# Packed blocks (100 sorted and 320 gathered steps a pass) and three loads of one-hot rows issued by ACT in the norm

## The chip, the core and the metric

The kernel runs on one core of a Trainium2 chip. The metric is the time of one execution on the device in microseconds. Before the change three runs gave a median of 2686.7 us (2684.65 to 2692.53). The profiled execution is a run of its own; profiles below are of it.

## What is computed

A graph of 3125 nodes with 128 features and 50000 edges, sorted by destination (the low nodes have far more edges than the high ones). First five steps of a gated graph network with residual and layer norm, then three edge layers with a residual and a layer norm:

```python
def _gnn_layer(edge_index, x, edge_attr, norm, We, be, Wn, bn):
    src, dst = (edge_index[0], edge_index[1])
    parts = [x[src], x[dst]]
    if edge_attr is not None:
        parts.append(edge_attr)
    e = jax.nn.relu(jnp.concatenate(parts, axis=-1) @ We + be)
    msg = e * norm[:, None] if norm is not None else e
    agg = jax.ops.segment_sum(msg, dst, num_segments=x.shape[0])
    x_new = jax.nn.relu(jnp.concatenate([x, agg], axis=-1) @ Wn + bn)
    return (x_new, e)
...
x = _layernorm(x + _L0_gnn_ref(x, ...))     # 5 gated steps, messages over the same edges
x = _layernorm(x + _L1_gnn_ref(...))        # three _gnn_layer; the edge rows e feed the next
```

## The kernel before, in words

The nodes lie in 25 windows of 128. The edge list is cut into 416 steps of 128 edges. The first 112 steps (`SORT_STEPS`), which hold edges of the crowded low windows, are sorted on the chip into blocks, one block for each pair of a source window and a destination window; the other 304 steps stay as they are. Every stage is a block of its own, with its work written out per engine; semaphores (`wait_ge`, `then_inc`) order it.

**Tables** (`step_tables`, `sort_on_dve`, `sort_on_pe`, 0 to 70 us). DVE and PE work out, for each edge of the 112 steps, its place among the blocks. A block takes whole tiles of 128 places. PE adds the first place of the block for each edge with 25 products in `row_of` (L543), DVE multiplies by the mask of the edge's block (L336) and sums over the windows (L340). The lists of windows of the 152 tiles (`SORT_TILES`) go to `list_i`.

**Adjacency** (`build_adjacency`, 70 to 375 us). POOL scatters a record of each edge of the sorted steps to its place in DRAM (L625), one scatter a step, in the pace of PE's products of the adjacency. Then five gated steps (`gated_steps`, to 940 us) and the norm (`add_and_norm`, to 965 us).

**First node stage** (`node_stage`, 965 to 998 us). It makes the node products P and Q of the first edge layer, kept in SBUF in three bfloat16 parts, P also in DRAM (`p_dram`). Here SP also loads the tables (L1236), and `hot_all`, the destinations of the gathered steps broadcast to all partitions, in four chunks (`load_hot`, L1225; quads 0, 8, 24, 48 and 76 bound them), the first of them ahead of the node products, the other three behind the stores of P. The rows of the sorted tiles are turned (L1287) and stored in `sorted_rows`.

**Edge pass** (`edge_pass`, three times, 998, 1560 and 2158 us). A slot is a quad of four tiles or steps, in the order sorted, gathered, gathered, and so on: 38 sorted and 76 gathered slots. For a slot

- POOL gathers the rows of P of a gathered quad from DRAM, four indirect DMAs (L1496), into one of seven row buffers (`ROW_SLOTS`); for a buffer that was used it waits for the slot sum that read it (`summed`, of L1607). SP loads `pair_rows` of a sorted quad (L1511), and in passes 1 and 2 the edge rows of the pass before (L1516).
- PE makes the edge rows in PSUM: Q by one-hot products of three parts (L1585), for a sorted slot also P (L1578), in passes 1 and 2 the edge rows by w_c (L1589).
- DVE adds the gathered rows (L1714), ACT takes the relu (L1657).
- PE turns the rows (L1600; ACT takes them at L1663, SP stores them at L1536, passes 0 and 1 only) and sums them into windows with weighted one-hots (L1607); DVE adds these sums to the window's column of `agg_t` (L1721).
- DVE makes the one-hots: `pair_hot` from bytes (L1695), `hot_all` in place (L1688, first pass), `hot_w` (L1705).

PE's order is the products of slot q, then turn and sum of slot q - 1. DVE's order is the add of slot q (or the `pair_hot` of the next sorted slot), then per tile the sum of slot q - 1 (L1721) and the weighted one-hot of slot q + 1 (L1705). PE and DVE load the window numbers of three slots at a time into registers. Behind the slots a loop treats tiles that didn't fit into the 152; its body runs once though there are none (L1503 gathers for it). The node stage of the layer follows.

The pace of a gathered slot is in these lines:

```python
def lists(i, first, engine):
    ...keep["list_i"][0:1, i, first:4 * QUAD]...
for q in range(SLOTS):
    if q % 3 == 0:
        values = lists(q // 3, 0, mybir.EngineType.PE)
    products(q, values)
    if q >= 1:
        turn_and_sum(q - 1)
```

## Time and profile before

| | us |
|---|---|
| median of three runs | 2686.7 |
| the profiled execution's own time | 2711.26 |
| its span in the trace | 2709.1 |
| tables | 0 to 70 |
| adjacency | 70 to 375 |
| gated steps and norm | 375 to 965 |
| first node stage | 965 to 998 |
| edge pass 0, with its loop for the rest | 998 to 1515 |
| edge pass 1 | 1560 to 2110 |
| edge pass 2 | 2158 to 2669 |
| last norm | 2669 to 2709 |

The node stages of 45 us lie between the passes. Over the span PE is busy 78%, DVE 53%, POOL 39%, ACT 25%; the mean over stages with such different work says little of any of them. How to read the rows below: a row of a timeline has its start, its length, engine, line and operation, tiles, a count, and in brackets the idle time of the engine ahead of it with what ended it; a row of groups has the busy time, the mean in ns, the idle time and the releaser. "issue" is time in which the engine waited for nothing that the profile shows.

### The profile page before, as it was taken

To read this page: it belongs to the slowest core of one execution; us is meant where nothing else is said; L and a number is where in the kernel's file an instruction comes from. 1 tells how busy PE (TensorE), PEld (TensorE's weight loads), DVE (VectorE), ACT (ScalarE), POOL (GpSimd) and SP (SyncE) were. 2 spreads that over 40 slices of the span, in tenths; PEclk is the share of its full clock that TensorE was granted. 3 is DMA by queue.
4 is the path that set the end of the run, shared out by engine and by line. 5 is a ranking of instruction groups with operands and counts; after the bars stand their busy time and mean duration, and the time that the engine had idled before them with its cause. 6 is when DMAs were issued, how large, how long until landed. Compare 5 with 4: busy or idle time off the path is not lost. (4 is left out here: it accounts for less than half of the span.)

```text
span 2709.1 us, 50361 instructions
## 1 busy us (share of the span) xinstructions
PE 2123.5 (78%) x14516; PEld 1514.4 (56%) x14516; DVE 1447.8 (53%) x4548; ACT 675.5 (25%) x1344; POOL 1068.0 (39%) x1086
## 2 busy tenths in 40 slices
PE   7777769999999726777777558888889458888885
PEld 5112124444444425666776348877878357777773
DVE  6888751322323255666666425555556336566565
ACT  0245751221212131222222312222222301111111
POOL 0544410000000035666664165555553266666650
PEclk7667779999999867889788769999999679999997
DMA  2023560000000043434443135555554134444431
GB/s 80 21 59 72 88 64 1 0 0 0 0 0 0 24 175 116 119 115 118 116 117 110 46 107 166 167 166 166 170 168 159 53 88 115 117 118 117 120 110 38
DMA packets 188937, 242.82 MB, mean 90 GB/s; under 512 B 53218, under 2 KB 115069, under 8 KB 188077
## 3 DMA queue, kind: packets, MB, share of 16 engines
q1 hardware_dynamic: 155852, 179.60, 22.9%
q0 software_dynamic: 32864, 60.32, 9.3%
q8 instruction: 135, 2.21, 0.3%
q14 instruction: 86, 0.70, 0.1%
HBM read 150.92 MB, written 69.26 MB: 81 GB/s over the span
## 5 line engine op out<-in xcount | busy, mean ns | idle before, releaser
L1496 POOL DMA_INDIRECT rows<-p_dram,src_i x912 | 899.4, 986 | 561.1 <-PE psum L1607 230.5
L1721 DVE TENSOR_TENSOR agg_t<-psum,agg_t 128x128 f32 x1368 | 390.8, 286 | 493.9 <-PE psum L1607 208.2
L1589 PE MATMUL psum<-w_c,before 128*128 128x128 f32 x1824 | 419.3, 310 | 18.9 <-issue 18.6
L882 PE MATMUL psum<-adj,parts 128*128 (+2 forms) x1750 | 340.0, 352 | 5.3 <-ACT agg L961 4.4
L1705 DVE TENSOR_SCALAR hot_w<-col_f,dst_loc,weight 128x128 f32<-128x128 f32 x912 | 323.9, 357 | 0.3
L1657 ACT ACTIVATE rows<-rows 128x512 f32<-128x512 f32 x228 | 143.6, 630 | 720.1 <-DVE rows L1714 459.7
L1585 PE MATMUL psum<-q_parts,hot_all 128*128 x2736 | 283.4, 221 | 29.3 <-issue 28.4
L1589 PEld LDWEIGHTS psum<-w_c,before 128*128 128x128 f32 x1824 | 289.3, 199 | 22.2 <-issue 22.2
L662 PE MATMUL psum<-src_hot,dst_hot 128*128 128x391 f16 x586 | 230.7, 439 | 77.5 <-ACT psum L684 26.7
L1607 PE MATMUL psum<-hot_w,rows 128*128 128x128 f32 x1824 | 270.2, 292 | 26.5 <-issue 24.9
L1578 PE MATMUL psum<-p_parts,pair_hot 128*128 x1368 | 194.2, 245 | 105.5 <-DMA before<-e_dram 49.4
L1262 POOL MEMSET agg_t<- 128x3200 f32 x3 | 8.3, 2765 | 664.4 <-POOLq L1010 607.4
L1607 PEld LDWEIGHTS psum<-hot_w,rows 128*128 128x128 f32 x1824 | 243.4, 205 | 33.8 <-issue 30.3
L882 PEld LDWEIGHTS psum<-adj,parts 128*128 128x128 f16 x1750 | 153.2, 98 | 190.9 <-issue 23.7
L1585 PEld LDWEIGHTS psum<-q_parts,hot_all 128*128 128x128 bf16 x2736 | 219.6, 99 | 51.9 <-issue 39.4
L1585 PE MATMUL psum<-q_parts,pair_hot 128*128 x1368 | 225.5, 246 | 15.6 <-issue 14.9
L1714 DVE TENSOR_TENSOR rows<-psum,rows 128x512 f32<-128x512 f32 x228 | 156.6, 687 | 138.5 <-remote 119.9
L1578 PEld LDWEIGHTS psum<-p_parts,pair_hot 128*128 128x128 bf16 x1368 | 134.5, 109 | 140.3 <-issue 121.8
L830 DVE SCALAR_TENSOR_TENSOR gate_room<-psum,b_h,gate_room 128x512 f32<-128x512 f32 (+1 forms) x35 | 23.9, 683 | 348.9 <-ACT gate_room L968 348.9
L662 PEld LDWEIGHTS psum<-src_hot,dst_hot 128*128 128x128 f16 x586 | 59.2, 101 | 249.1 <-issue 249.1
L644 DVE TENSOR_SCALAR src_hot<-gate_room 128x391 f16<-128x391 f16 x586 | 167.7, 332 | 53.2 <-PE psum L662 39.9
L625 POOL DMA_INDIRECT records<-record_of,place_i x112 | 125.6, 1122 | 158.6 <-PE psum L662 158.1
(248 smaller groups left out, 2547.2 us busy)
## 6 DMA issues: line engine op xcount, KB each, us to landing
e_dram<-after SPq DMA_DIRECT2D x228, 256.0 KB
before<-e_dram SPq DMA_DIRECT2D x228, 256.0 KB
adj<-stage SPq DMA_DIRECT2D x196, 97.8 KB
pair_rows<-sorted_rows SPq DMA_DIRECT2D x114, 128.0 KB
rows<-p_dram,src_i POOLq DMA_INDIRECT x912
hot_all<-dst_rows SPq DMA_DIRECT2D x1, 3584.0 KB
hot_all<-dst_rows SPq DMA_DIRECT2D x1, 3072.0 KB
hot_all<-dst_rows SPq DMA_DIRECT2D x1, 2048.0 KB, 7.5
```

The costliest lines, as they stand in the source:

```text
L644: nc.vector.tensor_scalar(src_hot[:, s % MOVES, :], span_h, place_f[:, s:s + 1], None, ALU.is_equal).then_inc(src_on, 1)
L662: nc.tensor.matmul(psum[:, bass.ds(bank, 1), 0:SPAN], dst_hot[:, s // HOT_BATCH % BATCHES, s % HOT_BATCH, :], src_hot[:, s % MOVES, :], st ...
L882: mm = nc.tensor.matmul(psum[:, AGG_BANK, 0:n_cols], parts[:, w, part, :], adj[:, w, cols], start=(w == 0 and part == 0), stop=(w == WINDO ...
L1496: nc.gpsimd.indirect_dma_start(out=rows[:, b % ROWS, m * D:(m + 1) * D], out_offset=None, in_=p_dram, in_offset=bass.IndirectOffsetOnAxis( ...
L1578: nc.tensor.matmul(o, hots[0], t["p_parts"][:, bass.ds(values[m], 1), part, :], start=(part == 0), stop=False)
L1585: mm = nc.tensor.matmul(o, hot, t["q_parts"][:, bass.ds(window, 1), part, :], start=(part == 0 and i is None), stop=(part == 2 and e_befor ...
L1589: mm = nc.tensor.matmul(o, before[:, q % BEFORE, m * P:(m + 1) * P], w_c[:], start=False, stop=True)
L1607: mm = nc.tensor.matmul(psum[:, A_BANKS[q % len(A_BANKS)], m * P:(m + 1) * P], e[:, m * D:(m + 1) * D], hot_w[:, q % 2, m, :], start=True, ...
L1657: nc.scalar.activation(e_of(q), source, ACT.Relu).then_inc(e_on, 1)
L1705: nc.vector.tensor_scalar(hot_w[:, q % 2, m, :], keep["col_f"][:], of, weight, ALU.is_equal, ALU.mult).then_inc(hot_on, 1)
L1714: nc.vector.tensor_tensor(row, psum[:, E_BANKS[q % len(E_BANKS)], 0:WIDE], row, ALU.add).then_inc(added, 1)
L1721: nc.vector.tensor_tensor(a, psum[:, A_BANKS[q % len(A_BANKS)], m * P:(m + 1) * P], a, ALU.add).then_inc(agg_on, 1)
```

## The change

Before, each block took whole tiles, so many tiles were half empty. Now a block takes (size + 64) >> 7 tiles; the edges past its full tiles (at most 64 of a block) go, packed one behind the other, to 8 tiles of their own (`LEFT_TILES`), which are gathered as ordinary steps are. Sorted steps are 104, sorted tiles 100 (25 slots), gathered steps 320 (80 slots): 105 slots a pass. Each edge now has two keys to look up, start and rank in one, fill and place of the leftovers in the other, so the products with `row_of` and the sum over windows are made twice, with some 22 further small operations on DVE. The record has its source too (four fields are read back), from which the leftovers' tables come.

In the edge pass the order follows from the counts: a sorted slot stands wherever q * 25 mod 105 is below 25, then three or four gathered slots follow. Windows are loaded for two sorted or four gathered slots at a time. Chunks 0 to 2 of `hot_all` are issued by ACT in the norm, behind its first square root; the last chunk (32 quads, 4 MB) stays with SP behind the stores of P, and now waits for the leftovers' rows.

```diff
-SORT_STEPS = 112
-SORT_QUADS = 38
+SORT_STEPS = 104
+SORT_QUADS = 25
 SORT_TILES = SORT_QUADS * QUAD
-REST_STEPS = STEPS - SORT_STEPS
+LEFT_TILES = 8
+HELD_TILES = LEFT_TILES + SORT_TILES
+FULL_FROM = 64
+REST_STEPS = STEPS - SORT_STEPS + LEFT_TILES
 REST_QUADS = REST_STEPS // QUAD
 SLOTS = SORT_QUADS + REST_QUADS
-ALL_TILES = 737
+ALL_TILES = 236
+RANKS, FILLS = 14, 9
...
+            sizes = psum[0:W, SORT_BANK, 64:64 + 2 * W]
+            after(nc.vector.tensor_scalar(tiles_i[0:W, :], sizes, float(P - FULL_FROM), None, ALU.add))
             after(nc.vector.tensor_scalar(tiles_i[0:W, :], tiles_i[0:W, :], 7, None, ALU.logical_shift_right))
             after(nc.vector.tensor_copy(tiles_f[0:W, :], tiles_i[0:W, :]))
-            v.on(nc.vector.tensor_reduce(row_tiles[0:W, :], tiles_f[0:W, 0:W], AXIS_X, ALU.add))
+            after(nc.vector.scalar_tensor_tensor(out=left[0:W, :], in0=tiles_f[0:W, :], scalar=-float(P), in1=sizes,
+                                                 op0=ALU.mult, op1=ALU.add))
+            after(nc.vector.tensor_scalar(left[0:W, :], left[0:W, :], 0.0, None, ALU.max))
+            v.on(nc.vector.tensor_reduce(row_sums[0:W, 0:1], tiles_f[0:W, 0:W], AXIS_X, ALU.add))
+            after(nc.vector.tensor_reduce(row_sums[0:W, 1:2], left[0:W, 0:W], AXIS_X, ALU.add))
...
+            chains = -(-W // CHAINED)
+            for key in range(2):
+                if key:
+                    dve.wait_ge(vec, done["rank_key0"])
+                for i, a in enumerate(range(0, W, CHAINED)):
+                    n = min(CHAINED, W - a)
+                    dve.wait_ge(ranked, key * chains + i + 1)
+                    done["chain", key, i] = v.on(nc.vector.tensor_tensor(
+                        block_rank[:, a:a + n, :],
+                        psum[:, (key * chains + i) % CHAIN_BANKS, 0:n * S].rearrange("p (k s) -> p k s", s=S),
+                        in_block[:, a:a + n, :], ALU.mult))
+                dve.wait_ge(vec, v.n)
+                done[f"rank_key{key}"] = v.on(nc.vector.tensor_reduce(
+                    rank_key[:, key, :], block_rank[:].rearrange("p k s -> p s k"), AXIS_X, ALU.add))
...
+            start_i, rank_i, left_at, fill_i = (split_i[:, i, :] for i in range(4))
+            v.on(nc.vector.tensor_scalar(start_i, key_i[:, 0, :], RANKS, None, ALU.logical_shift_right))
+            v.on(nc.vector.tensor_scalar(rank_i, key_i[:, 0, :], (1 << RANKS) - 1, None, ALU.bitwise_and))
+            v.on(nc.vector.tensor_scalar(left_at, key_i[:, 1, :], FILLS, None, ALU.logical_shift_right))
+            after(nc.vector.tensor_scalar(fill_i, key_i[:, 1, :], (1 << FILLS) - 1, None, ALU.bitwise_and))
+
+            v.on(nc.vector.tensor_tensor(base[:], base[:], start_i, ALU.subtract))
...
+            for key in range(2):
+                for i in range(chains):
+                    a, n, _ = below(i)
+                    j = key * chains + i
+                    if j >= CHAIN_BANKS:
+                        pe.wait_ge(vec, done["chain", (j - CHAIN_BANKS) // chains, (j - CHAIN_BANKS) % chains])
+                    for k in range(n):
+                        mm = nc.tensor.matmul(psum[:, j % CHAIN_BANKS, k * S:(k + 1) * S], row_of[:, a + k, :],
+                                              step_base[0:W, key, :], start=(key == 1), stop=(key == 1 or k == n - 1))
+                    mm.then_inc(ranked, 1)
...
+def load_hot(engine, hot_all, hot_in, dst_rows, i):
+
+    a, b = HOT_CHUNKS[i] * QUAD * P, HOT_CHUNKS[i + 1] * QUAD * P
+    skip = SORT_STEPS * P
+    engine.dma_start(hot_all[:, a:b], dst_rows[skip + a:skip + b].rearrange("(a n) -> a n", a=1)
+                     .broadcast_to([P, b - a])).then_inc(hot_in[i], 16)
+
...
                 nc.scalar.activation(spread[:, ts], spread[:, ts], ACT.Sqrt).then_inc(rooted, 1)
+                if b == 0 and dst_rows is not None:
+                    for i in range(len(HOT_CHUNKS) - 2):
+                        load_hot(nc.scalar, keep["hot_all"], keep["hot_in"], dst_rows, i)
...
-                load_hot(sp, 0)
+                    sp.dma_start(to[:, 0:STEPS - SORT_STEPS], tables[i][:, SORT_STEPS:STEPS]).then_inc(tabs, 16)
                 sp.wait_ge(turned_on, 2)
-                sp.dma_start(t["sorted_rows"][0:P, :, :], turned_rows[:, 0, :, :]).then_inc(tabs, 16)
-                sp.dma_start(t["sorted_rows"][P:SORT_TILES, :, :],
-                             turned_rows[0:SORT_TILES - P, 1, :, :]).then_inc(tabs, 16)
+                sp.dma_start(t["sorted_rows"], turned_rows[LEFT_TILES:HELD_TILES, :, :]).then_inc(tabs, 16)
+                sp.dma_start(dst_rows[STEPS * P:(STEPS + LEFT_TILES) * P].rearrange("(r p) -> r p", p=P),
+                             left_rows[:]).then_inc(tabs, 16)
...
-                    for i in range(1, len(HOT_CHUNKS) - 1):
-                        load_hot(sp, i)
+                    sp.wait_ge(tabs, 80)
+                    load_hot(sp, t["hot_all"], t["hot_in"], dst_rows, len(HOT_CHUNKS) - 2)
...
+                dve.wait_ge(keep["sorted_got"], 16)
+                for to, f in ((t["src_i"], 3), (t["dst_loc"], 1), (t["weight"], 2)):
+                    nc.vector.tensor_copy(to[:, STEPS - SORT_STEPS:REST_STEPS],
+                                          keep["sorted_in"][:, 0:LEFT_TILES, f]).then_inc(turned_on, 1)
...
+        order, nth_of = [], []
+        for q in range(SLOTS):
+            kind = q * SORT_QUADS % SLOTS < SORT_QUADS
+            nth_of.append(order.count(kind))
+            order.append(kind)
+        slots = {kind: [q for q in range(SLOTS) if order[q] == kind] for kind in (True, False)}
+        AT_A_TIME = {True: 2, False: 4}
+
         def sorted_of(q):
 
-            return q // 3 if q % 3 == 0 else None
+            return nth_of[q] if order[q] else None
 
         def rest_of(q):
 
-            return q // 3 * 2 + q % 3 - 1
+            return nth_of[q]
 
         def slot_of(b):
 
-            return b // 2 * 3 + b % 2 + 1
-
-        def lists(i, first, engine):
-
-            _, values = nc.values_load_multi_w_load_instructions(
-                keep["list_i"][0:1, i, first:4 * QUAD], engines=(engine,), min_val=0, max_val=WINDOWS - 1,
-                skip_runtime_bounds_check_because="a window's number is a count of at most all the windows but one")
-            return values
+            return slots[False][b]
+
+        def pair_slot(i):
+
+            return slots[True][i]
+
+        def lists(values, q, engine):
+
+            i, n = nth_of[q], AT_A_TIME[order[q]]
+            if i % n == 0:
+                if order[q]:
+                    table = keep["pair_i"][0:1, i:min(i + n, SORT_QUADS), :, :].rearrange("p i f m -> p (i f m)")
+                else:
+                    table = keep["rest_i"][0:1, i * QUAD:min(i + n, REST_QUADS) * QUAD]
+                _, values[order[q]] = nc.values_load_multi_w_load_instructions(
+                    table, engines=(engine,), min_val=0, max_val=WINDOWS - 1,
+                    skip_runtime_bounds_check_because="a window's number is a count of at most all the windows but one")
+            per = 2 * QUAD if order[q] else QUAD
+            return values[order[q]][i % n * per:(i % n + 1) * per]
 
...
             for q in range(SLOTS):
-                if q % 3 == 0:
-                    values = lists(q // 3, 0, mybir.EngineType.PE)
-                products(q, values)
+                products(q, lists(loaded, q, mybir.EngineType.PE))
```

## Rows read from the trace of the kernel before

**Rows 1.** The page's groups: the gather line; busy, mean ns, then idle and releaser.
```profile
L1496 POOL DMA_INDIRECT rows<-p_dram,src_i x912 | 899.4, 986 | 561.1 <-PE psum L1607 230.5
```

**Rows 2.** Windows, steady part of each pass: us, PE PEld DVE ACT POOL busy, PEclk, DMA, GB/s.
```profile
1036.40:1473.00 436.60, 334.53 (x2954) 301.82 (x2955) 282.58 (x1007) 120.19 (x211) 276.35 (x276) 0.86 0.40 116
...
1600.20:2067.00 466.80, 409.28 (x3725) 373.42 (x3726) 263.35 (x937) 116.72 (x208) 269.47 (x276) 0.96 0.56 167
...
2197.50:2631.60 434.10, 359.77 (x3341) 321.10 (x3341) 262.94 (x937) 64.39 (x104) 272.73 (x276) 0.99 0.41 116
```

**Rows 3.** Timeline of POOL, steady part of pass 0: first gathers of quads, one longer.
```profile
1205.43 0.94 POOL L1496 DMA_INDIRECT rows<-p_dram,src_i  x1 [1.56 <-PE psum L1607]
...
1207.91 1.40 POOL L1496 DMA_INDIRECT rows<-p_dram,src_i  x1 [0.30 <-issue]
...
1211.61 0.94 POOL L1496 DMA_INDIRECT rows<-p_dram,src_i  x1 [1.04 <-PE psum L1607]
...
1217.90 0.94 POOL L1496 DMA_INDIRECT rows<-p_dram,src_i  x1 [1.59 <-PE psum L1607]
```

**Rows 4.** The gather line behind the first 28, pass 0, 1 and 2.
```profile
L1496 POOL DMA_INDIRECT rows<-p_dram,src_i x276: 938/944/1402, 1043.5 to 1472.1; - x138
...
L1496 POOL DMA_INDIRECT rows<-p_dram,src_i x276: 938/944/1432, 1604.9 to 2066.1; - x138
...
L1496 POOL DMA_INDIRECT rows<-p_dram,src_i x276: 938/944/1499, 2201.6 to 2630.6; - x138
```

**Rows 5.** Timelines at the start of pass 2: PE, POOL, DVE.
```profile
2186.79 2.08 PE L1607 MATMUL psum<-hot_w,own 128*128 128x128 f32 x8 [15.96 <-issue]
...
2191.87 0.94 POOL L1496 DMA_INDIRECT rows<-p_dram,src_i  x1 [0.30 <-issue]
...
2197.49 0.69 DVE L1714 TENSOR_TENSOR rows<-psum,rows 128x512 f32<-128x512 f32 x1 [33.51 <-remote]
```

**Rows 6.** Timeline of DVE, steady part of pass 0.
```profile
1207.76 0.74 DVE L1695 TENSOR_SCALAR pair_hot<-pair_rows,lane_f 128x1024 bf16<-128x1024 uint8 x1
1211.48 0.29 DVE L1721 TENSOR_TENSOR agg_t<-psum,agg_t 128x128 f32 x1 [2.98 <-PE psum L1607]
```

**Rows 7.** Timeline of ACT's relus behind the last gather, pass 0, then pass 2.
```profile
1482.53 0.60 ACT L1657 ACTIVATE own<-psum 128x512 f32<-128x512 f32 x1 [2.31 <-PE psum L1585]
...
1486.88 0.63 ACT L1657 ACTIVATE rows<-rows 128x512 f32<-128x512 f32 x1 [2.95 <-DVE rows L1714]
...
1489.55 0.63 ACT L1657 ACTIVATE rows<-rows 128x512 f32<-128x512 f32 x1 [1.56 <-DVE rows L1714]
...
1492.36 0.60 ACT L1657 ACTIVATE own<-psum 128x512 f32<-128x512 f32 x1 [1.69 <-PE psum L1585]
...
2641.32 0.60 ACT L1657 ACTIVATE own<-psum 128x512 f32<-128x512 f32 x1 [2.45 <-PE psum L1589]
...
2650.53 0.60 ACT L1657 ACTIVATE own<-psum 128x512 f32<-128x512 f32 x1 [2.28 <-PE psum L1589]
```

**Rows 8.** Timelines of the tables stage: DVE's small operations, PE's chain, DVE's reduction.
```profile
48.71 0.18 DVE L315 TENSOR_SCALAR tiles_i<-tiles_i 25x50 int32<-25x50 int32 x1
48.92 0.18 DVE L316 CAST tiles_f<-tiles_i 25x50 f32<-25x50 int32 x1
...
52.35 11.00 PE L543 MATMUL psum<-step_base,row_of 25*128 25x112 f32 x50 [0.35 <-DVE step_base L327]
...
63.80 4.85 DVE L340 TENSOR_REDUCE place<-block_rank 128x112 f32<-128x2800 f32 x1
```

**Rows 9.** Timelines at the start of pass 0: SP's issues, POOL, DVE.
```profile
994.10 1.29 SPq L1225 DMA_DIRECT2D hot_all<-dst_rows  x3
...
998.40 0.99 POOL L1496 DMA_INDIRECT rows<-p_dram,src_i  x1 [1.90 <-POOLq L142]
...
1021.28 0.75 DVE L1695 TENSOR_SCALAR pair_hot<-pair_rows,lane_f 128x1024 bf16<-128x1024 uint8 x1 [25.95 <-DMA pair_rows<-sorted_rows]
...
1036.41 0.69 DVE L1714 TENSOR_TENSOR rows<-psum,rows 128x512 f32<-128x512 f32 x1 [11.14 <-PE psum L1585]
```

## Prediction of the time after

> **What bounds the kernel now.** I began with the groups of the page, to see which line of the three edge passes has most time to its name. It is the gather, L1496: 912 instructions of 0.99 us, and POOL idle most often for the slot sums of PE, L1607 [rows 1]. The three edge passes hold 1,330 of the 2,709 us in their steady parts alone [rows 2], so their pace is the question. I read it as the time from one quad of gathers to the next. In pass 0 the gathers behind the first 28 start from 1043.5 to 1472.1 us; less the three steps inside the last quad (some 4.2 us) that is 424.4 us for 68 steps, 6.24 us a quad. The same sum gives 6.73 in pass 1 and 6.25 in pass 2 [rows 4].
>
> The third view is POOL's timeline in the middle of pass 0 [rows 3]. Four gathers follow each other at 1.25 us; then POOL waits for a ring slot, which L1607 gives back: 1.56 us, 1.04 us, 1.59 us. Reader, note the period: 1205.43 to 1211.61 is 6.18 us, 1211.61 to 1217.90 is 6.29 us, and the two take three slots, one of them sorted. So POOL waits for its consumers, though by its own time it could do a quad in 5.0 us.
>
> But the consumers are not simply slow. Behind the last gather they need less: in the tail of pass 0 sorted slots come at 1482.53 and 1492.36, 9.83 us for the three slots that took 12.46 us beside gathers, and in the tail of pass 2 9.21 us [rows 7]. Nor does PE's work set the pace: pass 2 has 360 us of PE work in its steady part against 335 in pass 0, and the quads are equally long [rows 2, 4]. What holds them is seen at the start of pass 2: while POOL issues its first 28 gathers without a wait, PE stands for 15.96 us with nothing to wait for in the profile, and the first add of DVE starts at 2197.49, 4.7 us after the last of these gathers (2191.87, 0.94 long) [rows 5]. In the steady part DVE waits 2.98 us for a sum, until 1211.48, 0.9 us after the last gather of the quad before (1207.91, then one more of 1.25 to some 1210.6) [rows 3, 6]. So results of PE come through late while POOL issues gathers, and in a burst behind each quad. POOL waits for that burst in turn. The pace of a gathered quad is then its four gathers plus a wait for the burst, and only partly the slots' work. This is my reading, not something one row proves.
>
> **The change, part by part.** All is summed against the profiled run: span 2709.1 us, time 2711.26; the median of three runs is 2686.7, 0.9% lower. I add the difference to the median.
>
> *Slots.* 114 a pass become 105: 13 fewer sorted (38 to 25), 4 more gathered (76 to 80). Behind the free-running 28 gathers there were 68 intervals; there will be 72.
>
> What does an interval cost? The one from 1205.43 to 1211.61 holds a gather of 1.40 us in place of 0.94, beside the pair_hot of a sorted slot (1207.76, 0.74 us) [rows 3, 6]. Without it: 6.18 - 0.46 = 5.72. The pair of intervals was 12.47; less twice 5.72 leaves 1.03 for the one sorted slot (0.46 for the gather, 0.55 for the longer wait). After the change a gathered quad has 25/80 = 0.3125 sorted slots: 5.72 + 0.3125 x 1.03 = 6.04 us. Bounds: 5.4 (rival 2) and 6.24 (rival 1). Pass 0: 72 x 6.04 = 434.9 against 424.4, **+10.5**. Pass 2: against 425.0, **+10**.
>
> The Trainium skill, Advanced Engine Details and Errata, section Mode Summary, says that the second SBUF port of Vector is shared with GpSimd and that their instructions "will interfere/block eachother". The 1.40 us gather agrees; it prices nothing beyond that row.
>
> *Pass 1* reads and writes edge rows, and its 6.73 is above the others, so here the consumers' work counts too. In the tail of pass 0 a gathered slot follows a gathered one after 2.67 us (1486.88 to 1489.55); a sorted one costs 9.83 - 2 x 2.67 = 4.49 [rows 7]. A quad with its share of sorted slots falls from 2.67 + 0.5 x 4.49 = 4.92 to 4.07, by 0.84. 6.73 less 0.84 is 5.89, under the 6.04 of the other passes, which then holds. I take 6.15 (bounds 5.89 and 6.29): 72 x 6.15 = 442.8 against 457.3, **-14.5**.
>
> *Tails.* When the last quad's gathers are out, some 8 slots remain. Of the last 8 two were sorted, and one will be; one slot of 4.49 less, of which I take two thirds, since the remaining ones are staggered: -3 a pass, **-9** (bounds 0 and -13.5).
>
> *Tables.* The place of an edge now needs two keys. The 50 products of L543 took 11.00 us from 52.35, and the reduction L340 4.85 us behind them [rows 8]. The second key's 50 products run while the first is reduced, so PE is done 11 us later, and the second reduction starts that much later: +11. Behind and before it stand some 22 new small operations on DVE at 0.21 us from start to start (48.71 to 48.92), 4.6 us, a few of them under PE's products: +4. Sum **+15**, bounds +10 and +20; the next stage waits for it with nothing beside it. The scatters fall from 112 to 104, but they are paced by PE: 0.
>
> *Overflow.* The packed blocks drop remainders below 64 edges into 8 tiles that are gathered. Counting the drawn edges by the new rule gives 99 sorted tiles of 100 and 8 of 8; nothing overflows, as before, and the loop's one pass stays: 0.
>
> *Lists.* Loads of window numbers fall from 38 to 33 a pass on PE and DVE; they lie beside waits: 0.
>
> *Hot rows.* Chunks 0 to 2, some 6.3 MB, are issued by ACT behind the first root of the norm. Three issues took SP 1.29 us [rows 9]; on ACT the second root stands behind them, and who waits for that is DVE's scaling: 0 to +1.3. They left SP's queue ahead of pair_rows, for which DVE waited 25.95 us, until 1021.28 [rows 9]. That is freed; chunk 3, now 4 MB, is still ahead. What is late next? The first add came at 1036.41, 38.0 us after the first gather (998.40) [rows 9]; in pass 2, where no hot rows are loaded and pair_rows is not late, it came 39.4 us after it (the last of the 28 at 2191.87, less 27 x 1.25) [rows 5]. So the free run hides the load, and moving it gives **0**, bounds -12 (rival 3) and +2.
>
> Sum: 15 + 10.5 + 10 - 14.5 - 9 = +12: 2686.7 + 12 = **2699 us**. Own range of this case, from its terms' bounds: 2671 to 2725.
>
> **Rivals.**
> 1. *A fixed floor per gathered quad.* No mean of a pass is below 6.24, with quite different work beside it [rows 4]. If 6.24 is what four gathers and a burst cost whatever the slots hold, the four added quads are paid in full: 72 x 6.24 = 449.3, +25 in pass 0, +24 in pass 2, -8 in pass 1; with +15 and -9, +47: **2734**. Against it: the 0.46 us beside pair_hot is seen.
> 2. *Consumers set the pace, gathers only slow them: faster.* The three slots need 9.83 us alone and 12.46 beside eight gathers, 0.33 a gather [rows 3, 7]. After: 4.07 + 4 x 0.33 = 5.39 a quad, above POOL's own 5.0, so it decides: 72 x 5.39 = 388, -36, and as much in pass 1. In pass 2 the tail's 9.21 gives 0.41 a gather, a sorted slot of 3.87 and a quad of 5.5: 396, -29. With +15 and -9, -95: **2592**. For it: the ring of seven quads should absorb any delay that is not a rate, and pass 1 is slower where the work is more. Against it: the same rate carried from pass 0 to pass 2 gives 9.21 + 2.63 = 11.84 a group, and 12.5 is measured.
>    The Trainium skill, Perfetto Trace Analysis, on the SWDGE instruction, says that a GpSimd DMA's interval ends with its descriptors, not with the data's movement. By it the gather rows say nothing of when rows land; the 28 gathers of pass 2, whose consumers resume within 5 us of the last, show no later bound.
> 3. *Hot rows on time let pass 0 start early.* DVE's wait until 1021.28 ends 12 us before the last of the first 28 gathers ends; if PE is not held, these 12 us come off: 2699 - 12 = **2687**. Against it: pass 2.
> 4. The packing overflows on this data after all: some 10 us a tile and pass, from the idle time of the tail. The count of edges speaks against it.
>
> **How the numbers follow.** Forecast 0.42, rival 1 0.13, rival 2 0.28, rival 3 0.12, rival 4 and unnamed 0.05. The range must take in much of rival 2 and all but the end of rival 1: 2598 to 2738. What a measurement can tell from no change is about 0.3%, 8 us: 2679 to 2695. Slower: 0.26 of the forecast's 0.42, rival 1, and little else: 0.41. Faster: rival 2, and 0.07 of forecast and rival 3: 0.35. Same: 0.24.
>
> **What would show it.** Quads in pass 0 near 6.04 us: the forecast; near 6.24: rival 1; near 5.4, with POOL's waits gone from most quads: rival 2. The first add less than 34 us behind the first gather of pass 0: rival 3. The adjacency stage starting 15 us later, at some 85 us: the tables' term. Pass 1 still longer than pass 0 per quad by over 0.3 us would say its work term was too small. The forecast is wrong at its root if PE's late results beside gathers are a rate and not a burst, for then every slot saved counts.

## The result and the profile after

The change makes the kernel slower. Beside the kernel before at 2685.8 us it took 2764.9 us, a ratio of 1.0283 with a 95% interval of 1.0264 to 1.0302: +79 us, where +12 was forecast and the range ended at 2738 us. The profiled execution of the kernel after took 2756.73 us, span 2754.9.

The groups of the page of after, the gather line (in the page's columns of [rows 1]):

```profile
L1616 POOL DMA_INDIRECT rows<-p_dram,src_i x960 | 929.0, 968 | 573.7 <-issue 236.9
```

The gather line behind the first 28 gathers, passes 0, 1 and 2 of the kernel after, which answers [rows 4]:

```profile
L1616 POOL DMA_INDIRECT rows<-p_dram,src_i x292: 938/944/1487, 1059.2 to 1509.2; - x146
...
L1616 POOL DMA_INDIRECT rows<-p_dram,src_i x292: 938/944/1322, 1637.0 to 2087.7; - x146
...
L1616 POOL DMA_INDIRECT rows<-p_dram,src_i x292: 938/944/1500, 2215.3 to 2682.1; - x146
```

Read as before (first to last start, less the 3.7 to 4.2 us inside the last quad, by 72 steps) a quad takes 6.19, 6.20 and 6.43 us. Forecast were 6.04, 6.15 and 6.04.

Windows of the kernel after: up to the end of the tables, and the steady parts (us, busy us of PE, PEld, DVE, ACT, POOL, clock, DMA share, GB/s), which answer [rows 2]:

```profile
0.00:91.56 91.56, 65.40 (x287) 47.09 (x287) 61.82 (x165) 0.00 (x0) 3.44 (x15) 0.74 0.14 45
...
1059.20:1510.00 450.80, 316.49 (x2548) 276.80 (x2549) 260.08 (x929) 105.31 (x190) 281.85 (x292) 0.83 0.36 105
1636.50:2089.00 452.50, 377.07 (x3340) 335.46 (x3339) 239.85 (x855) 108.56 (x191) 282.67 (x292) 0.96 0.54 160
2215.30:2683.40 468.10, 369.64 (x2954) 329.00 (x2953) 241.41 (x856) 59.54 (x96) 282.77 (x292) 0.86 0.37 101
```

The windows of [rows 2] start at the first add; these start at the gather behind the first 28. The kernel before, pass 0, cut as here:

```profile
1043.50:1473.00 429.50, 327.96 (x2914) 295.32 (x2912) 278.77 (x995) 117.43 (x207) 276.35 (x276) 0.86 0.41 117
```

In pass 0 PE has 11 us less work than before in its steady part, DVE 19 less, and the part is 21 us longer. The engines that the packing relieves are not the ones that the time hangs on. One thing moves beside it: the granted TensorE clock of pass 2, a mean over the stretch, falls from 0.99 [rows 2] to 0.86, that of pass 0 from 0.86 to 0.83.

The tables, timelines of PE and DVE of the kernel after, which answer [rows 8]:

```profile
57.78 21.66 PE L635 MATMUL psum<-step_base,row_of 25*128 25x104 f32 x100 [0.46 <-DVE step_base L366]
...
69.18 5.07 DVE L388 TENSOR_REDUCE rank_key<-block_rank 128x104 f32<-128x2600 f32 x1
...
79.84 5.02 DVE L388 TENSOR_REDUCE rank_key<-block_rank 128x104 f32<-128x2600 f32 x1
...
91.60 1.22 DVE L731 TENSOR_TENSOR dst_hot<-gate_room 128x1024 f16<-128x1024 f16 x1 [0.33 <-PEq L163]
```

The next stage starts 21 us later (91.6 against 70.2), not 15: the products start 5.4 us later, the second key costs 10.7 us as forecast, and the small operations behind the second sum fill 6.4 us (84.9 to 91.3) where there had been 1.2.

POOL's timeline in pass 0 of the kernel after has another rhythm than [rows 3]:

```profile
1168.65 0.94 POOL L1616 DMA_INDIRECT rows<-p_dram,src_i  x1 [0.30 <-issue]
1171.65 0.94 POOL L1616 DMA_INDIRECT rows<-p_dram,src_i  x1 [2.06 <-remote]
...
1177.05 0.94 POOL L1616 DMA_INDIRECT rows<-p_dram,src_i  x1 [0.30 <-PE psum L1727]
...
1180.79 0.95 POOL L1616 DMA_INDIRECT rows<-p_dram,src_i  x1 [0.30 <-issue]
1187.69 0.94 POOL L1616 DMA_INDIRECT rows<-p_dram,src_i  x1 [5.95 <-PE psum L1727]
```

Eight gathers go out without a pause, and then POOL stands 6 us. While gathers go out, PE goes in small steps; its timeline near the start of pass 0:

```profile
1043.23 0.27 PE L1705 MATMUL psum<-q_parts,hot_all 128*128 x2
1045.34 0.27 PE L1705 MATMUL psum<-q_parts,hot_all 128*128 x2 [1.84 <-issue]
1046.74 0.22 PE L1705 MATMUL psum<-q_parts,hot_all 128*128 x1 [1.13 <-issue]
1048.17 0.26 PE L1705 MATMUL psum<-q_parts,hot_all 128*128 x1 [1.21 <-issue]
1049.57 0.26 PE L1705 MATMUL psum<-q_parts,hot_all 128*128 x1 [1.14 <-issue]
```

Nothing that the profile shows is waited for. The twelve products of one slot take nearly 16 us here (1043.23 to 1058.99). Nor are results there when PE's records say so. The sum of the first slot, and DVE's first add of it to the windows:

```profile
1037.61 1.91 PE L1727 MATMUL psum<-hot_w,own 128*128 128x128 f32 x8
...
1050.40 0.29 DVE L1840 TENSOR_TENSOR agg_t<-psum,agg_t 128x128 f32 x1 [9.06 <-remote]
```

That is 11 us behind the end of the records. Over all slots of pass 1 DVE's add starts 2.6 us (median) behind the end of PE's records of the slot sum in this trace and 1.6 us in that of the kernel before, against 0.15 us in the kernel without gathers (a_nogather, below).

### The profile page after: what moved, and what is told of

It is laid out like the page before. It is cut to its first block and busy times, and to the rows that moved or that the text cites. A ratio compares the mean times of both kernels' runs of the same rounds, so it can differ in the third digit from the quotient of the medians.

```text
span 2754.9 us, 46650 instructions
## 1 busy us (share of the span) xinstructions
PE 2097.5 (76%) x13351; PEld 1472.4 (53%) x13351; DVE 1396.3 (51%) x4356; ACT 648.8 (24%) x1299; POOL 1088.6 (40%) x1126
## 3 DMA queue, kind: packets, MB, share of 16 engines
q0 software_dynamic: 34144, 63.45, 9.7%
## 5 line engine op out<-in xcount | busy, mean ns | idle before, releaser
L1616 POOL DMA_INDIRECT rows<-p_dram,src_i x960 | 929.0, 968 | 573.7 <-issue 236.9
L1840 DVE TENSOR_TENSOR agg_t<-psum,agg_t 128x128 f32 x1260 | 357.1, 283 | 535.6 <-DMA records<-pad 171.6
L1705 PE MATMUL psum<-q_parts,hot_all 128*128 x2880 | 345.0, 240 | 121.3 <-issue 116.3
L1727 PE MATMUL psum<-hot_w,rows 128*128 128x128 f32 x1920 | 303.3, 297 | 69.5 <-issue 61.8
L1705 PEld LDWEIGHTS psum<-q_parts,hot_all 128*128 128x128 bf16 x2880 | 259.1, 109 | 178.3 <-issue 159.1
L1824 DVE TENSOR_SCALAR hot_w<-col_f,dst_loc,weight 128x128 f32<-128x128 f32 x960 | 337.0, 354 | 0.8
L1727 PEld LDWEIGHTS psum<-hot_w,rows 128*128 128x128 f32 x1920 | 267.4, 209 | 81.4 <-issue 70.4
L1709 PEld LDWEIGHTS psum<-w_c,before 128*128 128x128 f32 x1680 | 285.1, 211 | 47.8 <-issue 47.4
L738 DVE TENSOR_SCALAR src_hot<-gate_room 128x391 f16<-128x391 f16 x586 | 167.2, 330 | 53.9 <-PE psum L756 39.2
L1698 PE MATMUL psum<-p_parts,pair_hot 128*128 x900 | 118.1, 229 | 77.5 <-DVE pair_hot L1814 42.4
L1720 PE MATMUL psum<-ident,rows 128*128 128x128 f32 x640 | 111.0, 299 | 70.6 <-ACT rows L1776 49.5
L1776 ACT ACTIVATE own<-psum 128x512 f32<-128x512 f32 x75 | 44.8, 597 | 461.8 <-remote 381.9
```

The lines of the kernel that those rows point to most:

```text
L738: nc.vector.tensor_scalar(src_hot[:, s % MOVES, :], span_h, place_f[:, s:s + 1], None, ALU.is_equal).then_inc(src_on, 1)
L1616: nc.gpsimd.indirect_dma_start(out=rows[:, b % ROWS, m * D:(m + 1) * D], out_offset=None, in_=p_dram, in_offset=bass.IndirectOffsetOnAxis( ...
L1698: nc.tensor.matmul(o, hots[0], t["p_parts"][:, bass.ds(values[m], 1), part, :], start=(part == 0), stop=False)
L1705: mm = nc.tensor.matmul(o, hot, t["q_parts"][:, bass.ds(window, 1), part, :], start=(part == 0 and i is None), stop=(part == 2 and e_befor ...
L1709: mm = nc.tensor.matmul(o, before[:, q % BEFORE, m * P:(m + 1) * P], w_c[:], start=False, stop=True)
L1727: mm = nc.tensor.matmul(psum[:, A_BANKS[q % len(A_BANKS)], m * P:(m + 1) * P], e[:, m * D:(m + 1) * D], hot_w[:, q % 2, m, :], start=True, ...
```

## The experiments

Theories: **A**, gathers slow the consumers, so that a gathered quad has a price of its own, some 6.2 us, and sorted slots lie beside it for nothing (rival 1 of the prediction); **B**, the consumers' work sets the pace (rival 2); and, for what slows them, POOL running ahead, POOL's descriptors, the rows' landing, or PE's register work. The edits are against the kernel after (names a_) or before (b_). The runs met several chips, on which the kernel before took 2385 to 2715 us, so each run is read by its ratio to the kernel before on its own chip.

**Without gathers.** a_nogather and b_nogather:

```diff
+            nc.gpsimd.memset(rows[:], 0.0).then_inc(zeroed, 1)
+            pool.wait_ge(zeroed, 1)
             for b in range(REST_QUADS):
...
-                    nc.gpsimd.indirect_dma_start(...).then_inc(rows_in[b % ROWS], 16)
+                pool.sem_inc(rows_in[b % ROWS], 16 * QUAD)
```

The rows that are added are then not the right ones; no instruction of PE, DVE or ACT changes.

> The kernel after, with the gathers of the three passes left out (their rows are zero at the start of a pass and then what stands in the buffers; POOL only signals). Theory A, gathers slow the consumers: a gathered slot then costs 2.67 us and a sorted one 4.49 us, as in the tail, 80 x 2.67 + 25 x 4.49 = 326 us a pass in place of some 510, so about 2210 us in all. Theory B, the consumers are slow by their own work and gathers only fill their time: within 3% of the kernel after, 2680 to 2770 us.

> The kernel before, with the gathers of the three passes left out in the same way. Theory A: 76 x 2.67 + 38 x 4.49 = 374 us a pass in place of some 500, so about 2310 us, and then the kernel after without gathers would be about 100 us faster than this one, which is the work that packing saves. Theory B: 2600 to 2690 us.

Measured: 2195.8 and 2337.2 us, ratios of 0.810 (0.809 to 0.811) and 0.862 (0.860 to 0.863). Theory A's numbers (2210 and 2310 expected), and more: without gathers the packing would be worth 141 us, tables included. The work that it saves is real; the gathers take it back and 50 to 80 us beyond. From first to last add (the groups of DVE's adds in the timelines) the passes took 312, 348 and 303 us here against 359, 404 and 346 us in b_nogather. With 80 x G + 25 x S for the one and 76 x G + 38 x S for the other, a gathered slot is 2.5 us and a sorted one 4.4 us in pass 0: the tail's figures [rows 7] were right.

**The moved loads.** a_sphot:

```diff
-                if b == 0 and dst_rows is not None:
-                    for i in range(len(HOT_CHUNKS) - 2):
-                        load_hot(nc.scalar, keep["hot_all"], keep["hot_in"], dst_rows, i)
...
+                load_hot(sp, t["hot_all"], t["hot_in"], dst_rows, 0)
...
+                    for i in range(1, len(HOT_CHUNKS) - 2):
+                        load_hot(sp, t["hot_all"], t["hot_in"], dst_rows, i)
```

> The kernel after, with the one-hot chunks 0 to 2 issued by SP in the node stage again, as in the kernel before. Theory A, what is lost is lost in the steady parts of the passes: within 0.4% of the kernel after, 2755 to 2776 us, the first add of pass 0 some 17 us later and little else. Rival, the moved loads set off pass 0 in a bad rhythm: 2720 to 2745 us.

Measured: 2779.7 us, ratio 1.0246 (1.0226 to 1.0266). The rival, 2720 to 2745 us, falls: it isn't the moved loads that made the loss (the time is a little above theory A's 2755 to 2776). In its profile the eighth quad starts 44.6 us behind the first gather of pass 0; in the kernel after it is 39.3 us, 45.1 before. So they give pass 0 some 6 us. Its ratio isn't set against that of the kernel after, which was 1.028 on one chip and 1.021 on another.

**More sorted slots.** a_30:

```diff
-SORT_QUADS = 25
+SORT_QUADS = 30
```

> The kernel after with 30 sorted slots in place of 25 (the 5 added ones hold no edges), 110 slots a pass. Theory A with a floor per gathered quad: the added slots lie beside gathers, 2755 to 2780 us. Rival, every slot costs its work: 15 more slots of 4.49 us, 2825 to 2840 us. Should it be faster than the kernel after, then sorted slots between gathered ones are worth more than they cost.

Measured: 2764.3 us, ratio 1.0193 (1.0176 to 1.0210). Fifteen more slots cost nothing that shows; the kernel after is at 1.0206 or 1.0283, on other chips. B wanted +67 us.

**A smaller ring.** a_ring3:

```diff
-ROW_SLOTS = 7
+ROW_SLOTS = 3
```

> The kernel after with three row buffers in place of seven, so that POOL issues no gather further ahead than three quads and cannot issue two quads back to back while the consumers are behind. Theory A1, the loss is made by runs of gathers that POOL issues without a wait, which hold PE: 2680 to 2730 us on a chip where the kernel before has some 2700. Theory A2, each quad of four gathers costs its floor of some 6.2 us however far ahead it is issued: 2765 to 2800 us, within 1% of the kernel after.

Measured: 2735.6 us, ratio 1.0163 (1.0139 to 1.0187). Between the theories, and the profile says why: the gather line of pass 0 is

```profile
L1616 POOL DMA_INDIRECT rows<-p_dram,src_i x292: 941/947/1511, 1066.1 to 1517.1; - x146
```

which is 6.21 us a quad, as with seven. The pace doesn't hang on how far POOL runs ahead. What the small ring gives lies at the ends: the last add comes 5 us behind the last gather in place of 22, and the first add of pass 1 17 us behind the first gather in place of 40, since POOL's free run is 12 gathers and not 28. The three tails together are 16 us in place of 65; against that, from the first to the eighth quad the three passes take 148 us in place of 127.

**What it is about the gathers.** a_swdge, the indirect gather replaced by a plain load from POOL; a_hwdge, the same loads from SP, which waits for the slot sum in POOL's place (the edit shown is that of a_swdge):

```diff
-                    nc.gpsimd.indirect_dma_start(
-                        out=rows[:, b % ROWS, m * D:(m + 1) * D], out_offset=None, in_=p_dram,
-                        in_offset=bass.IndirectOffsetOnAxis(ap=t["src_i"][:, s:s + 1].bitcast(U32), axis=0),
-                    ).then_inc(rows_in[b % ROWS], 16)
+                    a = (b * QUAD + m) % 24 * P
+                    nc.gpsimd.dma_start(rows[:, b % ROWS, m * D:(m + 1) * D], p_dram[a:a + P, :]
+                                        ).then_inc(rows_in[b % ROWS], 16)
```

> The kernel after with the indirect gathers replaced by plain loads of 128 rows that POOL issues in the same places (the rows are the wrong ones, the bytes and destinations the same). If what slows the consumers is that POOL makes the descriptors, whatever the addresses: 2700 to 2790 us, as with gathers. If it is the indirect form alone (reading the list of indices, scattered rows): near the kernel without gathers, 2200 to 2300 us.

> The same plain loads, issued by SP instead of POOL; the bytes that land in the row buffers are as many. If the landing of the rows slows the consumers (queues, SBUF writes): over 2500 us. If it is POOL's making of descriptors: 2200 to 2350 us, near the kernel without gathers.

Measured: 2210.9 us, ratio 0.822 (0.821 to 0.824), and 2310.0 us, 0.859 (0.857 to 0.861). The first has the same queue, bytes and number of packets (q0: 34144 packets, 63.45 MB in both pages) and the same waits of POOL; only the indirect form is gone, and with it 550 us. So neither the landing of as many bytes nor the queue slows PE. A plain load reads 128 rows that lie together and an indirect one 128 scattered rows; list and scatter went together, and no run parts them. From SP it is 99 us slower, in passes 1 and 2, where SP also moves the edge rows.

a_static, constant windows in PE's products, so that PE has no register work and loads no lists there:

```diff
-                products(q, lists(loaded, q, mybir.EngineType.PE))
+                products(q, [m * 3 + q % 4 for m in range(2 * QUAD)])
```

> The kernel after with constant windows in PE's products of the edge passes (the sums are of wrong windows; PE loads no lists and does no register work there). If PE's slow steps beside gathers are its register instructions or its loads of lists: 2400 to 2650 us. If its matmuls themselves are slowed: within 2% of the kernel after, 2710 to 2790 us.

Measured: 2795.1 us, ratio 1.0391 (1.0373 to 1.0409). PE's timeline has the same steps:

```profile
1045.02 0.27 PE L1705 MATMUL psum<-q_parts,hot_all 128*128 128x128 bf16 x2 [1.19 <-issue]
1045.75 0.22 PE L1705 MATMUL psum<-q_parts,hot_all 128*128 128x128 bf16 x1 [0.45 <-issue]
1047.88 0.27 PE L1705 MATMUL psum<-q_parts,hot_all 128*128 128x128 bf16 x1 [1.91 <-issue]
```

So register work isn't the cause. That it got slower isn't explained, but the place is known: a quad takes 6.13, 6.97 and 6.36 us in the three passes, so the loss lies in pass 1, where the granted clock is 0.84 in place of 0.96.

**Both kernels on another chip.**

> The kernel before, unchanged, for a profile on the same chip as the others: 2685 to 2715 us; its quads at 6.1 to 6.3 us in passes 0 and 2, and pass 1 between 6.3 and 6.8 us, which is where a faster chip or run would differ.

> The kernel after, unchanged, beside its variants on one chip: 2.8% above the kernel before, as first measured (2750 to 2790 us). Of use for the variants' differences and for the profile.

Measured, on another chip than the runs above: 2385.3 us and 2423.4 us, ratio 1.0159 (1.0142 to 1.0176). Both expectations missed, by some 300 us: the same programs are 300 to 345 us faster here. The gather line of pass 0 of before and of after, behind the first 28 or 27, with what ended POOL's idle time:

```profile
L1496 POOL DMA_INDIRECT rows<-p_dram,src_i x276: 943/947/1448, 1037.3 to 1390.1; - x138
its engine sat idle before it (us, times) until:
  issue: 80.8, 265
  PE psum L1607: 3.4, 11
```
```profile
L1616 POOL DMA_INDIRECT rows<-p_dram,src_i x293: 940/944/1450, 1050.1 to 1423.6; - x147
its engine sat idle before it (us, times) until:
  issue: 85.1, 279
  PE psum L1727: 4.3, 14
```

A gather takes the same 0.94 us, but POOL hardly ever waits for PE and quads follow at 5.1 us. PE has no slow steps beyond those that it has without gathers: in the middle of pass 0 (ninth add to eighth from the end) it idles 31 times for 0.3 to 1.5 us, as in a_nogather, against 106 times in after_2 (below). The gathers' packets take as long on both chips (queue q0 of the pages: 9.7% of 2754.9 us, 11.2% of 2419.4 us), so it isn't the moving of the rows that differs.

Here POOL alone is the bound of the steady parts, but for pass 1 of before, where PE is busy for 357 of 358 us too. 68 quads of 5.13, 5.20 and 5.16 us become 72 of 5.12, 5.09 and 5.06: +46 us, where 12 quads of 5.1 would be +61. The tail of pass 1 falls from 27.0 to 3.0 us, and the first gather comes 14 us later. So the sorted slots taken away give 15 us in the steady parts and some 24 us of one tail.

**Four gathered slots fewer.** a_76 on this chip and a_76_2 on one of the first kind leave out the edges of the last 16 steps:

```diff
+        REST_QUADS = 76
+        SLOTS = SORT_QUADS + REST_QUADS
```

> The kernel after with 76 gathered slots a pass in place of 80 (the edges of the last 16 steps are left out), 101 slots. Floor theory, each gathered quad costs some 6.2 us whatever the sorted slots: 12 quads fewer, 74 us below the kernel after, 2680 to 2705 us where that has 2765. Work theory, a gathered slot costs its own 2.67 to 3.9 us: 32 to 47 us below, 2718 to 2733 us.

> The kernel after with 76 gathered slots in place of 80, once more. Where PE is slowed beside gathers the theory that each gathered quad has its price (6.2 us) gives 74 us below the kernel after, the theory that only the slots' own work counts some 30 us. Where PE isn't slowed: 60 to 63 us below, as before (12 quads of 5.1 us).

Measured: 2360.8 us where the kernel after has 2423.4 (-63 us, 5.2 a quad), and 2682.7 us where it has 2769.0 (-86 us, 7.2 a quad). On both kinds the number of gathered quads sets the time: neither number of the work theory is met (32 to 47 us, some 30 us). The 7.2 is above the 6.3 of a mean quad: pass 0 of a_76_2 also had 6.12 us a quad against 6.33.

**Half the gathers.** a_ind2, on the faster chip, and a_ind2_2, on a chip where the kernel before took 2715 us; every second gather is a plain load:

```diff
+                    if m % 2:
+                        a = s % 24 * P
+                        nc.gpsimd.dma_start(rows[:, b % ROWS, m * D:(m + 1) * D], p_dram[a:a + P, :]
+                                            ).then_inc(rows_in[b % ROWS], 16)
+                        continue
```

> The kernel after with every second gather replaced by POOL's plain load of 128 rows (the rows are the wrong ones). Without gathers it took some 2196 to 2211 us, with all some 2765 us. If each indirect gather has its price, 0.58 us: half way, 2450 to 2520 us. If gathers cost only once POOL's own time and its wait are longer than the consumers' work, nothing is left of it at half the number: 2200 to 2300 us.

> The kernel after with every second gather a plain load, once more, meant for a chip on which PE is slowed beside gathers. If each gather slows PE by itself (some 0.6 us each): 2450 to 2520 us. If only dense gathers do: 2200 to 2300 us, as on the chip where PE wasn't slowed (2210 us).

Measured: 2210.1 and 2207.8 us. On the first kind of chip too, nothing is left of the 550 us. POOL's timeline of a_ind2_2:

```profile
1201.83 0.98 POOL L1621 DMA_INDIRECT rows<-p_dram,src_i  x1 [0.30 <-issue]
1202.81 0.58 POOL L1618 DMA_DIRECT2D rows<-p_dram  x1
1203.70 0.97 POOL L1621 DMA_INDIRECT rows<-p_dram,src_i  x1 [0.30 <-issue]
1204.65 0.60 POOL L1618 DMA_DIRECT2D rows<-p_dram  x1
```

POOL is busy for a larger share than with all gathers (in the steady part of pass 0 232 of 285 us, against 282 of 451 in the kernel after), with an indirect gather every 1.9 us. So they cost PE nothing (the passes take 313, 356 and 303 us, without gathers 312, 348 and 303); at 1.25 us, one behind the other, they do on this chip's kind. It isn't a price for each gather. Whether it is the spacing or the plain load between them that helps, no run parts.

**Before and after on one chip of the first kind, and the ring of before.** b_ring3 is the edit of a_ring3 in the kernel before; b_ring3_hot, on yet another chip of this kind, has the moved loads besides.

> The kernel before, unchanged, for its profile beside the next ones. If the chip is one on which PE is slowed beside gathers: 2685 to 2715 us, quads of 6.1 to 6.3 us in passes 0 and 2. If it is one like the last, 2386 us and quads of 5.1 to 5.2 us.

> The kernel after, unchanged, beside it: 2.0 to 2.9% above the kernel before where PE is slowed beside gathers, 1.6% where it isn't. By parts, where PE is slowed: tables +21 us, 12 more gathered quads of 6.2 us +74 us, starts and tails of the passes -20 us; together +75 us.

> The kernel before with three row buffers in place of seven. POOL then stops after 12 gathers in place of 28 at a pass's start, and fewer slots are left at its end: where PE is slowed beside gathers, 25 to 35 us below the kernel before (the same edit took 1.2% from the kernel after); the pace of the quads between is unchanged at 6.24 us. Rival: a row buffer comes free too late with three, quads of 6.5 us and more, 30 us above. Where PE isn't slowed: within 0.3%.

> The kernel before with three row buffers and with chunks 0 to 2 of the one-hot rows issued by ACT in the norm: the two parts that cost nothing, without the packing. Where PE is slowed beside gathers: another 6 to 15 us below the kernel with three buffers alone, whose first ring release of pass 0 came 58 us after the first gather where the other passes had 49 to 51; so 1.4 to 1.8% below the kernel before. Rival, that load is hidden behind the gathers anyway: the same 1.2%. Where PE isn't slowed: within 0.5%.

Measured: before 2715.2, after 2769.0 us, ratio 1.0206 (1.0180 to 1.0232), so +54 us where the parts had been expected at +75; b_ring3 2680.0 us, 0.988 (0.985 to 0.991); b_ring3_hot 2675.5 us, 0.986 (0.983 to 0.988). The gather lines of passes 0, 1, 2 of before_2 and of after_2:

```profile
L1496 POOL DMA_INDIRECT rows<-p_dram,src_i x276: 938/944/1404, 1045.5 to 1474.1; - x138
...
L1496 POOL DMA_INDIRECT rows<-p_dram,src_i x276: 938/944/1421, 1606.6 to 2073.8; - x138
...
L1496 POOL DMA_INDIRECT rows<-p_dram,src_i x276: 938/944/1480, 2210.4 to 2639.5; - x138
```
```profile
L1616 POOL DMA_INDIRECT rows<-p_dram,src_i x292: 938/944/1509, 1057.3 to 1516.6; - x146
...
L1616 POOL DMA_INDIRECT rows<-p_dram,src_i x292: 938/944/1318, 1644.4 to 2102.1; - x146
...
L1616 POOL DMA_INDIRECT rows<-p_dram,src_i x292: 938/944/1319, 2230.5 to 2693.4; - x146
```

This is the fair pair for an account, of spans 2717.9 and 2768.2 us (differences from the unrounded times):

| part | before | after | difference, us |
|---|---|---|---|
| first gather of pass 0 | 1000.1 | 1018.0 | +17.9 |
| steady, pass 0 | 68 x 6.24 | 72 x 6.33 | +31.0 |
| steady, pass 1 | 68 x 6.82 | 72 x 6.30 | -9.8 |
| steady, pass 2 | 68 x 6.25 | 72 x 6.37 | +33.6 |
| start of pass 0, first to eighth quad | 45.4 | 39.2 | -6.2 |
| tails, last gather to last add | 26.2 + 29.4 + 25.9 | 22.3 + 22.9 + 21.0 | -15.2 |
| the rest | | | -1.0 |
| sum | | | +50.3 |

The granted clock of the steady parts was 0.86, 0.93 and 1.00 before and is 0.82, 0.96 and 0.89 after. In pass 2 it falls where PE has less to do, and a quad takes 0.12 us more. It doesn't set the pace by itself: in before a quad takes 6.24 us at 0.86 and 6.25 us at 1.00. But no run holds it fixed, so how much of the +33.6 is the clock's stays open.

With three buffers and without the packing the kernel is 1.2 to 1.4% faster than before on this kind of chip; that version beats both here. Whether the moved loads add to it the intervals don't tell (0.985 to 0.991 and 0.983 to 0.988 overlap), though the eighth quad of pass 0 starts 47.4 us behind the first in place of 58.5.

## Why the prediction was wrong, step by step

- **What bounds the kernel**: right. POOL's gathers and what they do to PE, not the slots' work, set the pace; the kernels without gathers and the second kind of chip show it. Late results of PE in a burst behind each quad was the reading of [rows 5, 6]; the traces bear out that they are late (the 2.6, 1.6 and 0.15 us above), and that of after shows PE itself in steps of 0.7 to 2.8 us while gathers go out. That they come in a burst behind each quad, no count shows.
- **The step that failed** is the price of a gathered quad, 5.72 + 0.3125 x 1.03 = 6.04 us; by it the three steady parts came to +6 us, and they measured +55. It took the 0.46 us of the gather beside pair_hot and the longer wait behind a sorted slot as things that go when the sorted slot goes. They don't: with fewer sorted slots the quads took 6.33, 6.30 and 6.37 us (6.19, 6.20 and 6.43 in the first profile), with more (a_30) 6.16, 6.38 and 6.39. The 5.72 itself was read from one interval; no pass of any run with all its gathers on these chips has a mean under 6.1. What POOL doesn't wait in one place it waits in another, as the 5.95 us behind eight gathers shows. Two neighbouring waits had been made into a law of slots. Rival 1, with 6.24, was the right mechanism, and its chance of 0.13 was far too low; the 0.28 of rival 2 belonged to it.
- **Pass 1**: 6.15 forecast, 6.20 and 6.30 measured, against 6.73 and 6.82 before; -14.5 forecast, -10 measured. Right in the main, and for the reason given: only there does the packing gain, until the quad is as long as in the other passes.
- **Pass 2** was the largest miss: +10 forecast, +34 measured. The prediction didn't ask what less work would do to PE's granted clock, which fell from 1.00 to 0.89 there; what that costs isn't shown.
- **Tables**: +15 forecast, +21 measured, above the bound of 20. The second key was right (10.7 us); the small operations ahead of the first product and behind the last sum came to 5.4 + 5.2 us where 4 were forecast: most wait for each other, and none of those was hidden.
- **Tails**: -9 forecast, -15 measured, a little beyond the bound of -13.5. **Moved loads**: 0 forecast, -6 measured; they let the consumers start 17 us earlier as rival 3 said (first add 20.5 us behind the first gather, against 38.0), and then two thirds of it were lost again, beside PE's slow steps: the second add came 18 us behind the first, against 5.
- **The sum**: by the account above +50, near rival 1's +47. That it comes so near is in part luck: its steady parts were +41 and measured +55, and tails and moved loads took that back. The "own range" up to 2725 is below what its terms' upper bounds add up to (+20, +25, +24, -4 and +2 give +67, so some 2754). The first measurement gave +79, with the kernel before at 2686 us there. On the chip of the account it took 2715 us, while the kernel after took 2765 and 2769 on the two. No profile of before is at hand from a chip where it takes 2686 us, so where those 25 to 30 us lie stays open. Nor did a range built on one chip's trace allow for it.

What stays open too is by what way dense indirect gathers slow PE, and why the runs on one chip are free of it. The runs rule out POOL's occupation, queue, bytes, packets, PE's register work and the distance ahead; what is left is the indirect form, with its list and its scattered rows, issued every 1.25 us.

## What to carry to other kernels

Ask of each unit of work what it costs the engine that sets the pace, not what it costs in all: the packing traded 13 slots that lay hidden for 4 that stood in the bound. Where two engines wait for each other, divide the time by the thing that the bound engine makes (here, quads), and test whether that figure holds when the other's work changes before building a sum on two neighbouring waits; here it held within 3% in passes 0 and 2. A deep ring isn't free: with seven buffers in place of three the quads between were as long and the kernel 1.2% slower, before and after. And compare on one chip: the ratio of these two kernels was 1.016, 1.021 and 1.028 on three.

## What the runs showed of the hardware

- Beside indirect gathers at 1.25 us spacing PE's matmuls come late on all chips met but one: the kernel after takes 2765 to 2769 us with them and 2196 us without; at 1.9 us spacing, with plain loads between, 2208 us. The Trainium skill, SBUF — State Buffer, section Who interferes with whom, holds that the ports shared by Vector and GpSimd are the only place of contention and that a DMA never contends with a compute engine; a_swdge (2211 us) agrees with it for plain loads; the runs with dense gathers (2765 to 2769 us) don't on these chips, though no trace shows where PE is held.
- Chips differ in this: the kernel before took 2385 us on one, met in one set of runs, and 2686 to 2715 us on the others, with gathers of the same 0.944 us and quads of 5.1 against 6.24 us. The kernel with half the gathers took 2210 and 2208 us on both kinds.
- A plain load of the same 64 KB takes POOL 0.55 us (529.3 us for 960 in a_swdge), and 28 of them go out in 15.6 us, with nothing between; a gather takes 0.944 us and 0.30 us stand between two.
